# Turning the second residual in transpose mode: rows and router columns as separate products in a fused vision block

## The reference

```python
h = _L0_tok_ref(x, W, b, cls_token, pos_enc)                 # patch embedding
h = h + _L0_attn_ref(_layernorm(h), ...)                     # running sums over tokens, rank 64
h = h + _L0_ffn_ref(_layernorm(h), ...)                      # 8 experts, top 2, capacity 185
```

## Time and profile before

| what | value |
|---|---|
| median of three runs | 158.98 us (158.18 to 159.10) |
| profiled execution, its own time | 158.09 us |
| its span, first to last instruction | 156.3 us |
| TensorE busy | 147.5 us (94%) |
| VectorE, ScalarE, GpSimd busy | 101.9, 80.3, 68.1 us |
| TensorE's share of the chain that ended last | 85% |

### The profile page before, as it was taken

One profiled execution on the slowest core, in us unless ns is written; L12 is line 12 of the kernel. 1 busy time (PEld: TensorE's weight loads), 2 busy tenths in 40 slices (PEclk: granted clock), 3 DMA queues, 4 the chain that ended last, 5 costly groups with the idle time before them and its releaser, 6 DMA issues.

```text
span 156.3 us, 2951 instructions
## 1 busy us (share of the span) xinstructions
PE 147.5 (94%) x980; PEld 138.7 (89%) x980; DVE 101.9 (65%) x321; ACT 80.3 (51%) x199; POOL 68.1 (44%) x78
## 2 busy tenths in 40 slices
PE   7999999999999988999999999999999999999950
PEld 7559999989889857999799999999999999999940
DVE  0057993669936697981498669479486694885710
ACT  4224755624342897656068366673773656737100
POOL 6002265675430740365438176084481761504361
PEclk9999999999999999999999999999999999999998
DMA  5999970079943375001207797879877889600421
GB/s 175 409 417 429 403 243 2 0 261 366 358 144 101 103 244 179 0 4 29 73 0 160 243 281 260 251 147 322 268 154 262 243 269 266 119 3 0 49 25 24
DMA packets 18242, 28.47 MB, mean 182 GB/s; under 512 B 1213, under 2 KB 14855, under 8 KB 17849
## 3 DMA queue, kind: packets, MB, share of 16 engines
q1 hardware_dynamic: 15769, 25.50, 47.3%
q0 software_dynamic: 2464, 2.86, 10.4%
HBM read 24.22 MB, written 4.14 MB: 181 GB/s over the span
## 4 chain that ended last, share of the span: by engine, by line
PE 85%; DVE 4%; issue 3%; ACT 2%; DMA 2%; POOL 1%; POOLq 1%; DVEq 0%
PE ps L1391 25%; PE ps L1426 12%; PE ps L1317 8%; PE ps L1206 6%; PE ps L1334 6%; PE ps L1428 5%; PE ps L1193 4%; PE ps L1246 4%; PE ps L1436 2%; PE ps L1218 2%; PE ps L1403 2%; DMA rows_in<-xrows,src_row 2%; PE ps L1378 2%; PE ps L1236 1%; PE ps L1292 1%
## 5 line engine op out<-in xcount | busy, mean ns | idle before, releaser
L588 POOL DMA_INDIRECT out_rows<-out_s,dst_row x16 | 23.8, 1488 | 38.0 <-ACT out_s L769 31.6
L745 ACT ACTIVATE first_t<-ps,b_cur 128x186 f32<-128x186 f32 x64 | 23.0, 413 | 22.8 <-PE ps L1391 21.7
L1426 PE MATMUL ps<-hid_hl,split 128*128 128x372 f32 x96 | 29.0, 369 | 0.0
L1428 PE MATMUL ps<-hid_hl,split 128*128 128x186 f32 x96 | 23.8, 248 | 0.0
L1391 PE MATMUL ps<-first_t,patch_t 128*128 128x186 f32 x128 | 21.7, 322 | 0.2 <-DVE first_t L1040 0.2
L1053 DVE CAST hid_hl<-first_t 128x372 fp32r<-128x372 f32 x28 | 10.7, 384 | 16.2 <-ACT first_t L745 16.1
L1391 PEld LDWEIGHTS ps<-first_t,patch_t 128*128 128x128 f32 x128 | 20.1, 189 | 0.5 <-issue 0.5
L573 POOL DMA_INDIRECT rows_in<-xrows,src_row x14 | 15.6, 1117 | 6.5 <-issue 4.0
L613 ACT ACTIVATE split<-patch_t 128x512 fp32r<-128x512 f32 (+2 forms) x28 | 14.3, 578 | 7.8 <-DMA patch_t<-patches 5.9
L1428 PEld LDWEIGHTS ps<-hid_hl,split 128*128 128x128 f32 x96 | 18.3, 191 | 0.0
L1426 PEld LDWEIGHTS ps<-hid_hl,split 128*128 128x128 f32 x96 | 18.0, 188 | 0.0
(11 more groups left out here) (187 smaller groups left out, 278.7 us busy)
## 6 DMA issues: line engine op xcount, KB each, us to landing
patch_t<-w SPq DMA_DIRECT2D x8, 1024.0 KB, 5.2
att<-w SPq DMA_DIRECT2D x3, 1024.0 KB, 5.3
h_t<-w SPq DMA_DIRECT2D x3, 1024.0 KB, 5.5
w_even<-w SPq DMA_DIRECT2D x2, 1024.0 KB, 17.3
att<-attn SPq DMA_DIRECT2D x1, 1281.0 KB, 8.8
patch_t<-patches SPq DMA_DIRECT2D x1, 1188.0 KB, 13.4
patch_t<-patches SPq DMA_DIRECT2D x1, 1080.0 KB, 10.9
first_t<-first SPq DMA_DIRECT2D x1, 978.0 KB, 6.2
```

Source lines behind the costliest of these rows:

```text
L588: pool.indirect_dma_start(out=out[:, :], out_offset=bass.IndirectOffsetOnAxis(ap=dst_row[0:SIZES[s], c:c + 1], axis=0), in_=out_s[q][0:SIZ ...
L745: ins = act.activation(hid[:, f, :], bank(UP_BANKS[pair])[:, (f % 2) * SL:(f % 2 + 1) * SL], ACT.Gelu, bias=b1_cur[q][:, f:f + 1])
L1426: pe.matmul(dst[:, 0:2 * SL], w2_h[q][:, f, cols], hid_hl[:, f].rearrange("p a s -> p (a s)"), start=f == 0, stop=False)
L1428: ins = pe.matmul(dst[:, 0:SL], w2_l[q][:, f, cols], hid_hl[:, f, 0], start=False, stop=f == KF - 1)
```

## The change

`mixed` goes. A new helper, `turn_into`, turns one half of a tile in transpose mode into its 128 columns, with the same half as stationary operand and the identity as moving operand, where these columns lie in one bank; where they cross a bank's end it calls `into_row` as before, so that a product with the identity stays, cut in two. The 9 router columns become a product of their own for each half, with `wr_c[k]` as moving operand. Both halves now add into the same nine columns in two products that start nothing. The sum with `prod` and `uw` stays as it is, and so do all waits.

```diff
-        mixed = [cst[:, C_ID.start:C_WR0.stop], cst[:, C_WR1.start:C_ID.stop]]
...
+            def turn_into(p, n, i, a, half):
+
+                r = rows_of(GROUPS[n][0] + i)
+                at = row_start(n, i) + a
+                if at // 512 < (at + HALF - 1) // 512:
+                    into_row(p, n, i, a, a + HALF, half, ident, first=True)
+                else:
+                    pe.matmul(p[0:r, at:at + HALF], half, ident, is_transpose=True, start=at % 512 == 0, stop=False,
+                              skip_group_check=True)
+
             def rows_summed(n):
...
                 for i, cols in tiles:
-                    into_row(p, n, i, 0, HALF + READ, hb_t[:, 0, cols], mixed[0], first=True)
-                    into_row(p, n, i, HALF, ROW, hb_t[:, 1, cols], mixed[1], first=True)
+                    for k in range(KD):
+                        turn_into(p, n, i, k * (HALF + READ), hb_t[:, k, cols])
+                        into_row(p, n, i, HALF, HALF + READ, hb_t[:, k, cols], wr_c[k])
                 drained(pe, "uw2", 0)
```

## The result

In 20 runs each the changed kernel takes 159.68 us and the kernel before 158.84 (medians). The ratio is 1.0071, with a 95% interval of 1.0053 to 1.0089: 1.13 us slower (0.84 to 1.41), against a forecast of +0.90. The two medians by themselves lie 0.84 us apart, at the low end of that interval. The profiled execution took 159.09 us with a span of 157.3, after 158.09 and 156.3.

A forecast was written before the change was run, and what follows sets the result against it. TensorE, busy 94% of the span, was taken to bound the kernel, with groups A and B on its chain. +0.45 us in each, C and E hidden, gave 158.98 + 0.90 = 159.9 us; range 158.8 to 161.3, 8 times in 10.

The forecast's parts named there:

- The chain: TensorE's rows of groups A and B lie on the critical chain, +0.45 us each; C and E do not.
- What was expected to be hidden: Growth of groups C and E on TensorE behind B, 0.10 us each, 0.20 in all.
- the wait of 0.69: TensorE's idle wait for B's choice, at 57.13 us, 0.69 us long, said to cover C's and E's growth.
- The count of records: First part of the groups on TensorE: 66 records instead of 44, 22 more.
- The price of a product of nine columns: Router products on TensorE: two fp32 weight loads of 0.11 us, 0.22 in all, nearly the old product's 0.23.
- The rival that took the pace of the short bf16 products: TensorE's small products at 0.047 us a record: 0.31 gained twice, 158.4 us; chance 0.10.
- The price of a transpose: Each transposed half on TensorE: 0.06 us, from the length of its load, between 0.03 and 0.11.
- The low end, 0.03: Cheapest transpose on TensorE, from five loads in 0.47 us at the folded factors; would make the change +0.60.
- Equal loads: Every TensorE load costs 0.11 us, the transposes' too: +0.70 in A and in B, 160.4 us; chance 0.20.
- The size: First part of a group of 3 on TensorE: 2.06 us in place of 1.61, +0.45; A and B together +0.90.
- The turns: Rival: TensorE drains between transposes and products, 0.08 us each, twenty in A and B, 161.5 us; chance 0.13.
- The clock: Rival: TensorE's clock falls to 1.2 GHz from A's to B's rows, 9.7 us doubled, 169.6 us; chance 0.02.

The follow-up runs named there:

- ab_only: The change in groups A and B alone, C and E keeping the products of 137 columns; ratio to the kernel before 1.0085 (1.0055 to 1.0116).
- ce_only: The change in groups C and E alone, A and B keeping the products of 137 columns; ratio to the kernel before 0.9975 (0.9950 to 1.0000).
- grouped: The changed kernel with all transposes and the cut product of a group ahead of its router products; ratio to the kernel before 1.0097 (1.0058 to 1.0135).
- fp32_apart: The changed kernel without transpose mode: identity always an fp32 product, router columns products of their own; ratio to the kernel before 1.0157 (1.0121 to 1.0193).

## Why the prediction was right, step by step

The time, 159.68, lies in the range and close to the forecast of 159.9. Part of that closeness is luck: the difference by the ratio is +1.13 and by the traces +1.08, both above the +0.90, while the kernel before came out at 158.84 in place of 158.98.

*The chain.* A's and B's rows carry the change, C's and E's are covered. Shown by ab_only and ce_only. The part behind the stretch kept its length within 0.25 us. What was expected to be hidden, 0.20 us, was 0.31; the wait of 0.69 held it.

*The count of records.* 44 became 66; the page has 980 and 1002.

*The price of a product of nine columns.* 0.22 was taken from four loads in 0.44. The twelve loads in grouped go at 0.11 each, and fp32_apart gives 0.116 over 26 loads with the streamed columns unchanged. This is the step on which the sign hung, and it held. The rival that took the pace of the short bf16 products falls with it.

*The price of a transpose.* Taken as 0.06 between 0.03 and 0.11; among products it is about 0.07, in a row 0.11 (grouped). The number was near, but the reason for it does not hold: it came from a transpose's load record being 50 ns shorter than a product's, and among products the transposes' load records last 0.23 us (41.57, 41.85), longer than the 0.14 there. So this term came out by luck. The low end, 0.03, was read up to the load behind the transpose (22.79), and what the transpose delays after that was left out. Equal loads, the rival at +1.40, gives +0.70 per group where the traces show +0.54; the measured time alone, +0.84 to +1.41, would not rule it out. The rule quoted from the Trainium skill ("TensorE: Matmul & The Clock Gate", section "LDWEIGHTS (loading the stationary operand)") makes the three loads of a half 0.32 us, an estimate from its formula: it agrees for products in a row, 0.11 a load, and not for a transpose between products, where the half takes 0.28 to 0.29.

*The size.* The sum was 0.18 short: +0.45 per group of 3, measured +0.54. From the first load of `hb_t` to the first of `uw` it is the same +0.54 (41.21 to 43.47, 2.26 us, after 41.54 to 43.26, 1.72), so all of it lies in the first part. With 0.07 for a transpose the sum is 16 x 0.11 + 5 x 0.07 = 2.11, +0.50; the 0.04 left is within the rounding of the load's price, which counts 16 times.

*The turns.* They cost nothing in full tiles, or grouped would have been faster. *The clock.* 1.00 through the stretch, with 18 transposes of the change in it.

## What to carry to other kernels

Count the weight loads before counting the streamed columns: here an fp32 product of 9 columns takes 0.22 us and one of 137 takes 0.23, so a few columns that ride in a product whose stationary operand is loaded anyway are almost free, and splitting them off costs a product. That price falls with the columns of the stationary operand: with 32 in place of 128 the records start 0.03 apart in place of 0.11, not counting the change of width ahead of them. A transpose is cheaper than an fp32 product with the identity (0.07 to 0.11 for 0.23), but only if nothing else then needs the same operand loaded again. Look for cuts at bank ends as well: a row of 265 columns cut into 137 and 128 costs less than one cut into 247 and 18 (2.96 us for 3.15 per group of 3).

## What the runs showed of the hardware that was not expected

A transpose record's cost depends on its neighbours: 0.11 us after another transpose, about 0.07 between products of nine columns.

The stretch ahead of the change, whose code is the same in all these kernels, varies by far more than the change: the 24 products of the first projection take 8.36 us on the chain of the changed kernel's execution, 8.62 in the kernel before and 9.73 in fp32_apart.

```profile
3.92 8.36 PE ps L1344 x24
```

```profile
3.93 9.73 PE ps L1344 x24
```

A's first record came at 41.42 us in one execution and at 42.67 in another. The spans of single profiled executions can therefore not be compared to a few tenths, which is why the stretch was measured from A's first record. The traces show where the difference arises: in fp32_apart this projection's products start 0.66 us apart until 6.7 us and 0.33 apart from 7.2 us on, in the changed kernel's execution 0.33 apart from 4.4 us on. The trace's record of the granted clock begins at 7.0 us in the one and at 4.2 in the other, at the level of 2.4 GHz. So a step to twice the pace comes at different moments; that it is the clock that rises from 1.2 GHz is inferred, since no clock is recorded ahead of the step (a view of windows there prints 1.00 for want of a record), and what sets the moment was not tried.
